# Weighing the recurrence's outputs on GpSimd instead of VectorE in the last routing stage

## The reference, cut to what matters

```python
o_flat = ((o - mu) * jax.lax.rsqrt(var + EPS)).reshape(Bn, Tn, C) * gn_weight + gn_bias
bonus = ((rh * kh * r_k).sum(-1, keepdims=True) * vh).reshape(Bn, Tn, C)
o_flat = o_flat + bonus
return o_flat * g @ W_o
...
x = x + _L0_attn_b_ref(_layernorm(x, axis=-1), ...)
# then the mixture: a second layer norm with gamma and beta, logits, the best expert of each
# token, its rank among the tokens of that expert, and a copy of the token into the expert's slot
logits = tokens.astype(jnp.float32) @ gate_weight.astype(jnp.float32).T
top1 = jnp.argmax(logits, axis=-1)
rank_e = jnp.cumsum(onehot, axis=0) - onehot
dispatch = dispatch.at[top1, slot].add(tokens * keep[:, None])
```

## Time and profile before

| | us |
|---|---|
| median of 3 runs | 4181.92 |
| lowest and highest of them | 4176.39, 4189.79 |
| the profiled execution | 4145.23 |
| its span | 4143.2 |
| last stage: from its first loads to the end of the scatters | about 3669 to 3880 |
| its steady batches | 3740 to 3854 |

### The profile page before, as it was taken

The page is one execution under the profiler, slowest core; times in us unless marked ns, Lnnn a source line. Parts: engine busy times, 40 slices in busy tenths (PEclk is TensorE's granted clock), DMA queues, the critical chain, the costliest instruction groups (busy, mean ns, idle before and its releaser), DMA issues. The chain is left out here.

```text
span 4143.2 us, 71975 instructions
## 1 busy us (share of the span) xinstructions
PE 3763.5 (91%) x23268; PEld 2624.9 (63%) x23268; DVE 3043.1 (73%) x8486; ACT 2309.5 (56%) x7477; POOL 2046.1 (49%) x1995
## 2 busy tenths in 40 slices
PE   5999999999999669699977999999999999958698
PEld 2344443444443646466656888888888888858465
DVE  4777778777774711178877999999999999959210
ACT  1666666666666611166751677677777777724211
POOL 2212112112212432222338999999999999803322
PEclk7999999999999679899988999999999999978799
DMA  4323323323234724234454233332333323158232
GB/s 114 85 61 93 85 69 88 86 69 93 67 78 89 248 66 136 77 138 192 183 208 54 36 46 39 44 46 37 46 42 41 46 37 46 23 182 295 66 118 81
DMA packets 466739, 378.13 MB, mean 91 GB/s; under 512 B 298860, under 2 KB 424585, under 8 KB 460228
## 3 DMA queue, kind: packets, MB, share of 16 engines
q1 hardware_dynamic: 454084, 348.38, 34.5%
q0 software_dynamic: 12288, 25.28, 1.8%
HBM read 221.61 MB, written 159.58 MB: 92 GB/s over the span
## 5 line engine op out<-in xcount | busy, mean ns | idle before, releaser
L750 DVE TENSOR_REDUCE at_neg_max<-at_slot 128x1 f32<-128x512 f32 (+3 forms) x1216 | 746.0, 656 | 246.6 <-PE at_slot L542 243.6
L672 ACT ACTIVATE at_prob<-at_slot 128x512 f32<-128x512 f32 (+1 forms) x1216 | 631.2, 577 | 353.7 <-PE at_slot L562 352.7
L2196 PE MATMUL sc_added<-sc_outer,sc_ident 128*128 128x128 f32 x4096 | 626.3, 276 | 47.7 <-POOL sc_outer L1919 47.7
L2216 PE MATMUL sc_ps_o<-sc_terms,sc_ident 128*128 128x256 f32 x2048 | 608.6, 381 | 2.4 <-DVE sc_o_buf L2005 2.4
L2036 DVE TENSOR_TENSOR sc_rank<-sc_u,sc_pack 128x128 f32<-128x128 f32 x2048 | 603.0, 294 | 0.0
L390 POOL TENSOR_SCALAR_AFFINE_SELECT at_prob<-at_prob 128x512 f32<-128x512 f32 x256 | 162.8, 636 | 886.2 <-ACT at_prob L672 886.0
L2023 DVE TENSOR_TENSOR sc_prod<-sc_state,sc_three 128x384 f32<-128x384 f32 x1024 | 571.6, 558 | 14.9 <-POOL sc_from_v L1913 14.9
L2196 PEld LDWEIGHTS sc_added<-sc_outer,sc_ident 128*128 128x128 f32 x4096 | 541.0, 192 | 48.5 <-issue 48.5
L2108 ACT ACTIVATE sc_seen<-sc_state 128x512 f32<-128x512 f32 x256 | 270.2, 1056 | 459.0 <-DVE sc_prod L2023 450.7
L1943 POOL TENSOR_TENSOR sc_terms<-sc_seen,sc_pack 128x1024 f32<-128x1024 f32 (+2 forms) x288 | 491.6, 1739 | 21.4 <-PE sc_ps_o L2216 20.7
L542 PE MATMUL at_slot<-at_k_stack,at_q_stack 96*128 96x512 bf16 (+3 forms) x1536 | 458.5, 334 | 20.8 <-DMA at_k_stack<-parts 19.7
(11 more groups left out here) (309 smaller groups left out, 6733.2 us busy)
## 6 DMA issues: line engine op xcount, KB each, us to landing
packed<-pr_pack SPq DMA_DIRECT2D x16, 3072.0 KB, 9.1
sc_pack<-packed SPq DMA_DIRECT2D x512, 96.0 KB, 3.7
parts<-at_parts SPq DMA_DIRECT2D x96, 256.0 KB
f_up_w<-in_ffn_wi SPq DMA_DIRECT2D x16, 1024.0 KB, 5.0
f_down_w<-in_ffn_wo SPq DMA_DIRECT2D x16, 1024.0 KB, 8.4
at_q_stack<-parts SPq DMA_DIRECT2D x32, 384.0 KB
at_k_stack<-parts SPq DMA_DIRECT2D x32, 384.0 KB
slots<-at_no_row SPq DMA_DIRECT2D x2, 4128.0 KB, 22.4
```

The lines of the kernel that those rows point to most:

```text
L672: act.activation(prob[:, first:first + n, q1 - tiles * P:q1], ps[:, 0:n * tiles * P].rearrange("p (n k) -> p n k", n=n), ACT.Exp)\
L750: dve.tensor_reduce(neg_max[:, chunk, qt, h:h + n], ps[:, 0:n * tiles * P].rearrange("p (n k) -> p n k", n=n), AX.X, ALU.max, negate=True) ...
L2196: pe.matmul(added[h][:, 0:HALF], ident[:], outer[m % 2][:, 2 * n + s, h * HALF:(h + 1) * HALF], start=(s == 0), stop=False)
L2216: last = pe.matmul(ps_o[m % 2][:], ident[:], by_column[:, n], start=first, stop=last_one)
```

## The change

For batches 1 to 7 POOL does both instructions of `weigh_o`, with the same operands. Batch 0 stays on DVE. POOL waits for the loads, multiplies, waits for its own product (`multiplied`), adds, and signals `pool_weighed`; PE waits for that in place of `weighed_o`. The list of jobs is unchanged, so on POOL `weigh_o` of batch b+1 stands in front of `place` of batch b-2.

```diff
@@ finish_and_route
+        multiplied = sem("multiplied")
+        pool_weighed = sem("pool_weighed")
@@ gpsimd
+            weight_wide = wide_w[:].unsqueeze(1).broadcast_to([P, TILES, C])
             for stage, what, s, use in plan.jobs:
-                if stage == "place":
+                if stage == "weigh_o" and what:
+                    k = what % 2
+                    pool.wait_ge(norm_in, 1 + 32)
+                    pool.wait_ge(in_ready[k], 1 + 48 * (what // 2 + 1))
+                    pool.tensor_tensor(o[k][:], o[k][:], weight_wide, ALU.mult).then_inc(multiplied, 1)
+                    pool.wait_ge(multiplied, 1 + what)
+                    pool.tensor_tensor(o[k][:], o[k][:], bonus[k][:], ALU.add).then_inc(pool_weighed, 1)
+                elif stage == "place":
@@ tensor
                     if (c, half) == (0, 0):
-                        pe.wait_ge(weighed_o, 1 + b + 1)
+                        if b:
+                            pe.wait_ge(pool_weighed, 1 + b)
+                        else:
+                            pe.wait_ge(weighed_o, 1 + 1)
@@ vector
                 if stage == "weigh_o":
-                    weigh_o(what)
                     if what == 0:
+                        weigh_o(what)
```

## The result

| | us |
|---|---|
| before, median of 13 runs | 4179.26 |
| changed, median of 13 runs (4187.48 to 4206.89) | 4196.16 |
| ratio, 95% interval | 1.0037, 1.0029 to 1.0044 |
| profiled execution of the changed kernel, its span | 4201.99, 4200.3 |
| last routing stage, from the first memset of POOL to the first memset of the experts' loop | 259.3, before 219.8 |

The forecast was +43 us; measured are +15.5 us by the ratio, +16.9 by the medians. Yet within the two profiles the stage grew by 39.6 us, nearly as forecast. The two do not contradict each other. The kernel before, unchanged, took 4144 to 4145 us on some occasions and 4179 to 4186 us on others, never both in the timed runs of one occasion; I call these the 4145 level and the 4180 level.

What follows compares the result with a forecast made beforehand. It took PE's 10.6 us plus DVE's 9.8 us per batch as the bound, the weighing hidden. Gain of 1.5 us, holds of 5 x 8.6 and PE's 1.5 gave +43 us on 4181.9: 4225 us, range 4186 to 4234.

Steps and rivals of the forecast that it cites:

- Bound of the steady batches, weighing worth 0: Last routing stage: PE's 10.6 us plus DVE's 9.8 us bound a batch; the weighing's 4.6 us lie beside PE's work.
- Part 1: Work leaving DVE: batches 2 to 7 gain 0; batch 1 lets r_turn start 1.5 us earlier, once.
- Part 2: Work added to POOL: seven pairs of 128x2048 instructions, 4.5 us each; POOL's 19.4 us cycle stays under the 20.44 us period.
- the bound of 3.67: Lower bound, in us, on one POOL weighing instruction, from a 2048-element instruction with repeated operands; 4.72 was the other bound.
- Part 3: POOL's two instructions each stop DVE's SBUF instructions for 4.3 us; f_tok of batches 1 to 5 loses 8.6 us each.
- The first hit: Batch 3's loads land near 3728.9; POOL's multiplication gets in before batch 1's last two or three f_tok; margin about 0.6 us.
- This then repeats: With f_tok held, the store leaves early, loads land 17.5 us after it, and the next f_tok is held too: 5 x 8.6 us.
- The term for PE's idleness: PE's transposes run slower after longer idling before r_turn: 0.3 us for each of five batches, 1.5 us in all.
- The sum: Whole kernel: -1.5 + 5 x 8.6 = +41.5 us, plus 1.5 for PE, +43 us, added to the median 4181.9: 4225 us.
- held in some batches only: Rival, chance 0.12: the first hit is missed and later pairs drift into f_tok, 1 to 3 hits, +7 to +27 us, about 4200.

Runs made afterwards that it cites:

- unweighed: The kernel before with nobody weighing batches 1 to 7, norm's weight and bonus left out there: 4140.08 us against 4145.35, ratio 0.9988.
- after_look: The changed kernel, unchanged, profiled once more: 4177.07 us, where the kernel before took 4145.35 us (median of 15 runs).
- after_routed: The changed kernel, with POOL's two weighing instructions from batch 3 on also waiting for VectorE's f_send_to of an earlier batch: 4167.98 us against 4184.18 before, ratio 0.9961.
- after_third: The changed kernel, unchanged, timed again beside the kernel before: 4195.80 us against 4185.84, ratio 1.0026.

## Why the prediction was wrong, point by point

- **Bound of the steady batches, weighing worth 0: right**, by `unweighed`.
- **Part 1, -1.5 us once: right.** `f_tok` of batch 1 starts at 3726.67 in `after_look` and at 3728.8 in the profile of before, 2.1 us earlier.
- **Part 2, 4.5 us per POOL instruction: right** (4.49 to 4.61, and 4.89 where it first waited for an `f_tok`); the bound of 3.67 was never near.
- **Part 3, DVE's instructions stand still: right**, for 3.9 to 4.6 us each in batches 1 to 5 of the result's profile and of `after_look` (4.3 forecast). The Trainium skill, SBUF — State Buffer, "SBUF: two separate sides", calls it an exclusive lock for the whole instruction; the runs agree, `f_mine` and `f_earlier` above ending within 0.1 us of POOL's instruction. The list of what can be held, `f_roots` through `choose` to the last `f_tok` and three of `route`, was right too: even `f_roots` and the cast, with one input of 8 elements, are held; only the reductions and reciprocals among them are not. It left `bn_stats` out, rightly; my later expectation for `after_routed` took it in and was wrong by that.
- **The first hit: right in time, half in size.** The loads of batch 3 landed at 3728.8 in `after_look`, forecast 3728.9. But the multiplication got in before the last `f_tok`, not before the last two or three, so the addition met `gate_y`, which reads PSUM, and one hold of the two fell away.
- **"This then repeats": the step that failed.** I took the pair to fall on `f_tok` each time, 17.5 us after the last one, since the store leaves while `f_tok` is held. After batch 1 it did leave early (3730.91, `f_tok` held until 3733.52, SP timeline of `after_look`):

```profile
3730.91 0.38 SPq L1239 DMA_DIRECT2D out_x<-f_base  x1
3733.60 0.36 SPq L1219 DMA_DIRECT2D f_x<-x_mixed  x1
...
3764.55 0.38 SPq L1239 DMA_DIRECT2D out_x<-f_base  x1
3765.04 0.52 SPq L1219 DMA_DIRECT2D f_x<-x_mixed  x1
```

  But the next pair came 15.8 us after `f_tok`, not 17.5 (in `after_look` straight behind the scatters, at 3749.30), and so fell on `f_roots` and `choose`, ahead of `shift`. That costs the same two holds, but then ACT's `base` isn't ahead of a held `f_tok`: the store left at 3764.55, 1.6 us after `f_tok` had ended (3762.99), the loads landed at 3784.7, 21.7 us after it, and the pair missed batch 3's `f_tok` by 0.2 us:

```profile
3749.30 4.52 POOL L1272 TENSOR_TENSOR f_o<-f_o,f_wide_w 128x2048 f32<-128x2048 f32 x1
...
3784.85 4.54 POOL L1272 TENSOR_TENSOR f_o<-f_o,f_wide_w 128x2048 f32<-128x2048 f32 x1 [6.54 <-DMA f_og<-gate]
```

  Only batches 1, 2, 4 and 5 were held: 30 us and not 5 x 8.6 = 43.
- **The term for PE's idleness, 1.5 us: too small.** I took it from the 16 transposes, and they did take 3.65 us instead of 3.46. But `y_out` behind them took 3.5 us more over four batches of `after_look`, the granted clock being at 1.2 GHz into it.
- **The sum was put on a base it did not come from.** A profile 37 us below the median of its kernel is not that kernel, a little luckier: 17.6 us of the 37 lay in the very stage I was summing, 16.7 of them waits in front of `choose`. At the level of that profile the change costs 28 to 32 us, and the step above explains the miss; at the level of the median these waits get 8 to 9 us shorter in the changed kernel and the holds are fewer in two profiles of three (29.2, 23.0 and 20.2 us), and it pays 10 to 17 us. The second half of the miss is this step.
- **Rivals.** The measured time, 4196, is where "held in some batches only" (0.12, "about 4200") put it, and its idea, hits that are missed by a small margin, is what the profiles show. That its number fits is partly luck: it took the first hit as missed and 1 to 3 hits after it, +7 to +27 us. Four batches were held in the result's profile, the first hit among them, 29.2 us, and shorter waits that it did not have took 8.4 back. Only `after_third` went as the rival says. Its chance was taken from the margin of the first hit; the margins of the later ones weren't asked for.

**Open:** why PE's semaphores come late at the 4180 level, 2.4 to 5.1 us after the products in the kernel before, 1.5 to 4.1 in the changed one, and at other instructions with the pair behind `f_send_to`; and what sets the level. No row shows it; that the wait goes with VectorE's weighing is only a guess, which no run tested there.

## What to carry to other kernels

Moving work from VectorE to GpSimd is not free for VectorE even when it has no part in it: ask which VectorE instructions on the critical chain read SBUF alone, and start GpSimd's instruction by a semaphore that puts it beside those that read PSUM or take statistics, instead of letting a DMA's landing choose the moment. A saving that lies off the path still costs nothing only as long as its replacement stays off it. And when the profiled execution lies outside the range of the timed runs, find the stage in which they differ before a sum is added to the median. A wait whose printed releaser makes no sense is worth a look at the semaphore itself: it may be an engine whose rows have ended but whose word has not come.

## What the runs showed of the hardware that was not expected

- The same kernel has two levels 0.8 to 1.0% apart (medians of 4144 to 4145 us against 4179 to 4186), and the difference lies in the two routing stages: 129 to 131 against 143 to 148 us in the first, 219.6 to 219.8 against 237.4 in the last. It goes with PE's late semaphores, which only the 4180 level has.
- In the untouched stage it begins at the 4180 level with one period of 21.2 to 21.4 us, the fourth, then 13.3 to 13.5 us per batch, where the 4145 level has about 10.3. `after_routed` has a like one before batch 7's `f_tok`, 28.3 us: DVE waits 8.45 us for `y_out`, while PE's `gate` products come a few at a time with gaps marked "issue" and the DMA engines are busy for 0.03 of the time (3860 to 3870).

```profile
3861.87 0.51 PE L1346 MATMUL f_ps_gate<-f_gate_scaled,f_turned 128*128 128x8 f32 x4 [0.59 <-issue]
3863.30 0.41 PE L1346 MATMUL f_ps_gate<-f_gate_scaled,f_turned 128*128 128x8 f32 x3 [0.92 <-issue]
```

- Not held by a POOL instruction beside them: DVE's `bn_stats` (2.71 us for eight, beside the addition above), its aggregate, reductions (0.22), reciprocals, and everything with an input in PSUM (an add, 0.69). Held until POOL's instruction ended: tensor-scalar, cast, tensor-tensor and scalar-tensor-tensor with all inputs in SBUF, down to 8 elements.
